# Gate and up by seven block products in tapped PSUM chains, token pairs outermost

## The chip, the cores and the metric

The kernel runs on one core of one Trainium2 chip. The metric is the time of one execution on the device in microseconds (us); three runs of the kernel before gave 2370.25, 2370.45 and 2370.57 us, so the median is 2370.45 us. The core's engines work side by side, each on its own queue of instructions, in order: TensorE (PE, with its weight loads as PEld), VectorE (DVE), ScalarE (ACT), GpSimd (POOL) and SyncE (SP), which here issues the DMAs. They wait for each other through semaphores.

## The reference

A mixture of eight routed experts and one shared expert is added to its input. There are 16 sequences of 256 tokens, so 4096 tokens, of width 256, and each expert is 1024 wide.

```python
E, B, S, D, F = (8, 2, 256, 256, 1024)   # the real B is 16
g = jnp.einsum('bsd,edf->ebsf', h, Wg)
u = jnp.einsum('bsd,edf->ebsf', h, Wu)
expert_outs = jnp.einsum('ebsf,efd->ebsd', jax.nn.silu(g) * u, Wd)
expert_output = jnp.einsum('be,ebsd->bsd', gating_probs, expert_outs)
shared = jnp.einsum('bsf,fd->bsd', jax.nn.silu(h @ Sg) * (h @ Su), Sd)
sg = shared_gate_prob[:, :, None]
x = x + (1.0 - sg) * expert_output + sg * shared
```

All arrays are float32. The gate g and the up projection u use the same input h; silu(g) * u goes through the down projection, and the result is weighted with one number for each sequence and expert.

## The kernel before

**Tiles.** The 4096 tokens are 8 tiles of 512 tokens, held transposed (128 partitions of the width, two halves of it, 512 tokens). Nine experts (eight and the shared one) each have 8 chunks of 128 of their 1024 columns. One tile times one chunk is a unit of the work; there are 9 x 8 x 8 = 576 of them.

**Precision.** Each operand is kept as a high part (`w_hi`, `x_hi`, `h_hi`) and the rest (`w_lo`, `x_lo`, `h_lo`), each in the type fp32r. A `product` (lines 170 to 174) is three matmuls of a 128x128 stationary block with 512 moving columns: hi·hi, hi·lo and lo·hi.

**A unit** has two products for the gate (the two halves of the width), two for up, and two for down (the two halves of the output): 6 products, 18 matmuls. ACT applies silu to the gate in PSUM (`unit`, line 294), DVE multiplies with up in PSUM (line 397), ACT makes `h_hi` (line 300), DVE makes `h_lo` (line 404), and PE uses both in `down`.

**Order.** The loops run over the experts outermost and over the tiles within. PE's queue is written out by hand: `down` of a unit stands ahead of gate and up of the unit two later (`tile`, lines 210 to 219 and after), with two PSUM banks each for gate and up and four for down. The down sums of one tile and one expert stay in PSUM for 8 units; DVE then adds them to `acc` with the coefficient (`add_tile`, line 384). The weights of an expert are loaded once, 72 loads of 384 KB in all; ACT makes their hi (line 284) and DVE their lo (line 368) once each, 8 pairs per expert. POOL works only at the start: it makes hi and lo of the tiles 1 to 7 (lines 161 and 163). SP issues all large DMAs.

Of the kernel before, what the change touches and what calls it, by code (L numbers as in the profile page):

```python
# [5 lines left out]
F32 = mybir.dt.float32  # L25
# [6 lines left out]
S_BUFS = 2  # L32
H_BUFS = 4


def moe_kernel(nc, xT, w, probs, shared_gate, out):
# [4 lines left out]
    D = DC * P  # L41
    HALVES = BATCH // TILES
    SEQ = TOKENS // HALVES
    assert EXPERTS == ROUTED + 1 and W_COLS == 3 * D and TILES % 2 == 0 and HALVES * TILES == BATCH
    UNITS = TILES * CHUNKS
    PAIRS = (TILES - 2) // 2


    FREED = 2


    LEAD = 3
    GATE = slice(0, D)
    REST = slice(D, 3 * D)

    with ExitStack() as ctx:
# [8 lines left out]
        x_hi = sb("x_hi", [P, TILES, DC, TOKENS], F32R)  # L65
        x_lo = sb("x_lo", [P, TILES, DC, TOKENS], F32R)
        w_raw = sb("w_raw", [P, CHUNKS, W_COLS])
        w_hi = sb("w_hi", [P, CHUNKS, W_COLS], F32R)
        w_lo = sb("w_lo", [P, CHUNKS, W_COLS], F32R)
        silu = sb("silu", [P, S_BUFS, TOKENS])  # L70
        h = sb("h", [P, S_BUFS, TOKENS])
        h_hi = sb("h_hi", [P, H_BUFS, TOKENS], F32R)
        h_lo = sb("h_lo", [P, H_BUFS, TOKENS], F32R)
# [6 lines left out]
        gate_ps = ctx.enter_context(nc.psum_tensor("gate_ps", [P, 2, TOKENS], F32))  # L80
        up_ps = ctx.enter_context(nc.psum_tensor("up_ps", [P, 2, TOKENS], F32))
        down_ps = ctx.enter_context(nc.psum_tensor("down_ps", [P, 2, DC, TOKENS], F32))

        w0_gate_loaded = sem("w0_gate_loaded")
        x0_loaded = [sem(f"x0_loaded{c}") for c in range(DC)]
        w_loaded = [sem(f"w_loaded{k}") for k in range(CHUNKS)]
        x_loaded = [sem(f"x_loaded{t}") for t in range(1, TILES)]
        gates_loaded = sem("gates_loaded")
        stored = sem("stored")
        w_hi_done = sem("w_hi_done")  # L90
        w_split = sem("w_split")
        w0_gate_hi_done = sem("w0_gate_hi_done")
        w0_gate_split = sem("w0_gate_split")
        x0_hi_done = [sem(f"x0_hi_done{c}") for c in range(DC)]
        x0_split = sem("x0_split")
        x_hi_done = sem("x_hi_done")
        x_split = sem("x_split")

        gate_done = sem("gate_done")
        up_done = sem("up_done")  # L100
        down_done = sem("down_done")
        silu_done = sem("silu_done")
        prod_done = sem("prod_done")
        h_hi_done = sem("h_hi_done")
        h_split = sem("h_split")
        tile_added = sem("tile_added")
        last_sums = sem("last_sums")
        last_added = sem("last_added")
# [5 lines left out]


        @block.sync
        def _(sp):
            def load_weights(e, k):
                sp.dma_start(w_raw[:, k, :], w[e, k]).then_inc(w_loaded[k], 16)

            def load_tokens(t):
                sp.dma_start(acc[:, t], xT[t]).then_inc(x_loaded[t - 1], 16)


            sp.dma_start(acc[:, 0, 0, :], xT[0, :, 0, :]).then_inc(x0_loaded[0], 16)
            sp.dma_start(w_raw[:, 0, GATE], w[0, 0, :, GATE]).then_inc(w0_gate_loaded, 16)
            for c in range(1, DC):
                sp.dma_start(acc[:, 0, c, :], xT[0, :, c, :]).then_inc(x0_loaded[c], 16)
            sp.dma_start(w_raw[:, 0, REST], w[0, 0, :, REST]).then_inc(w_loaded[0], 16)
            for k in range(1, CHUNKS):  # L130
                load_weights(0, k)
            for t in range(1, TILES):
                load_tokens(t)
            with sp.Fori(1, EXPERTS) as e:
                for k in range(CHUNKS):

                    sp.wait_ge(w_split, (e - 1) * CHUNKS + k + 1)
                    sp.dma_start(
                        w_raw[:, k, :], w[bass.ds(e, 1), k, :, :].rearrange("a p c -> (a p) c")
                    ).then_inc(w_loaded[k], 16)  # L140
            with sp.Fori(0, TILES - 1) as t:

                sp.wait_ge(tile_added, (EXPERTS - 1) * TILES + 1 + t)
                sp.dma_start(
                    out[bass.ds(t, 1)].rearrange("a p c n -> (a p) c n"),
                    acc[:, bass.ds(t, 1)].rearrange("p a c n -> p (a c) n"),
                ).then_inc(stored, 16)
            for c in range(DC):

                sp.wait_ge(last_added, c + 1)  # L150
                sp.dma_start(out[TILES - 1, :, c, :], acc[:, TILES - 1, c, :]).then_inc(stored, 16)
            sp.wait_ge(stored, 16 * (TILES - 1 + DC))


        @block.gpsimd
        def _(pool):
            pool.dma_start(probs_sb[:], probs.partition_broadcast(P)).then_inc(gates_loaded, 16)
            pool.dma_start(shared_sb[:], shared_gate.partition_broadcast(P)).then_inc(gates_loaded, 16)
            for t in range(1, TILES):
                pool.wait_ge(x_loaded[t - 1], 16)  # L160
                nc.gpsimd.tensor_copy(x_hi[:, t], acc[:, t]).then_inc(x_hi_done, 1)
                pool.wait_ge(x_hi_done, t)
                nc.gpsimd.tensor_tensor(
                    x_lo[:, t], acc[:, t], x_hi[:, t].bitcast(F32), ALU.subtract
                ).then_inc(x_split, 1)


        @block.tensor
        def _(pe):
            def product(out_ps, k, cols, moving_hi, moving_lo, start, stop):  # L170

                nc.tensor.matmul(out_ps, w_hi[:, k, cols], moving_hi, start=start, stop=False)  # L172
                nc.tensor.matmul(out_ps, w_hi[:, k, cols], moving_lo, start=False, stop=False)  # L173
                return nc.tensor.matmul(out_ps, w_lo[:, k, cols], moving_hi, start=False, stop=stop)  # L174

            def tile_x(t):

                if isinstance(t, int):
                    return [(x_hi[:, t, c, :], x_lo[:, t, c, :]) for c in range(DC)]
                return [  # L180
                    tuple(x[:, bass.ds(t, 1), c, :].rearrange("p a n -> p (a n)") for x in (x_hi, x_lo))
                    for c in range(DC)
                ]

            def first_gate():

                g = gate_ps[:, 0, :]
                for c in range(DC):
                    cols = slice(c * P, (c + 1) * P)
                    if c == 0:  # L190
                        pe.wait_ge(w0_gate_hi_done, 1)
                    pe.wait_ge(x0_hi_done[c], 1)
                    nc.tensor.matmul(g, w_hi[:, 0, cols], x_hi[:, 0, c, :], start=(c == 0), stop=False)
                    pe.wait_ge(x0_split, c + 1)
                    nc.tensor.matmul(g, w_hi[:, 0, cols], x_lo[:, 0, c, :], start=False, stop=False)
                pe.wait_ge(w0_gate_split, 1)
                for c in range(DC):
                    cols = slice(c * P, (c + 1) * P)
                    last = nc.tensor.matmul(g, w_lo[:, 0, cols], x_hi[:, 0, c, :], start=False, stop=(c == DC - 1))
                last.then_inc(gate_done, 1)  # L200

            def gate_up(e, T, k, x, wait_banks=True, only_up=False):


                pe.wait_ge(w_split, e * CHUNKS + k + 1)
                sides = ((gate_ps, 0, gate_done, silu_done), (up_ps, D, up_done, prod_done))
                for ps, column0, done, used in sides[1:] if only_up else sides:
                    if wait_banks:

                        pe.wait_ge(used, T * CHUNKS + k - 1)  # L210
                    for c in range(DC):
                        cols = slice(column0 + c * P, column0 + (c + 1) * P)
                        last = product(ps[:, k % 2, :], k, cols, *x[c], start=(c == 0), stop=(c == DC - 1))
                    last.then_inc(done, 1)

            def down(T, k, parity, very_last=False):


                pe.wait_ge(h_split, T * CHUNKS + k + 1)
                for c in range(DC):  # L220
                    cols = slice(2 * D + c * P, 2 * D + (c + 1) * P)
                    last = product(
                        down_ps[:, parity, c, :], k, cols, h_hi[:, k % H_BUFS, :], h_lo[:, k % H_BUFS, :],
                        start=(k == 0), stop=(k == CHUNKS - 1),
                    )
                    if very_last and c < DC - 1:
                        last.then_inc(last_sums, 1)
                last.then_inc(down_done, 1)
# [301 lines left out]
```

## Time and profile before

| what | value |
|---|---|
| median of the timed runs | 2370.45 us |
| span of the profiled execution, first to last instruction | 2368.9 us |
| outside that span, by the median | 1.55 us |
| PE busy | 2355.2 us, 99% |
| DVE busy | 973.8 us, 41% |
| ACT busy | 757.2 us, 32% |
| POOL busy | 30.3 us, 1% |
| granted TensorE clock, mean | 1.000 |

The profiled execution has no time of its own beside its span; the runs were timed apart, within 0.32 us of each other. Matmuls overlap, so the row of one shows 0.39 us while they start 0.227 us apart: the distance of the starts is what one costs. A row of a DVE or ACT instruction likewise overlaps the next on its engine by 0.08 to 0.10 us.

### The profile page before, as it was taken

How to read it: one execution, taken by the hardware profiler on the slowest of the kernel's cores; microseconds unless marked ns; L12 is line 12 of the kernel's file. 1: busy time of each engine (PE TensorE's matmuls, PEld its weight loads, DVE VectorE, ACT ScalarE, POOL GpSimd, SP SyncE). 2: the span in 40 equal slices, each digit the busy share in tenths (PEclk: the TensorE clock that was granted, in tenths of full speed). 3: DMA queues.
4: the chain of work that ended last, by engine and by line, in shares of the span. 5: the costliest groups of instructions: out<-in, count | busy, mean ns of one | idle time of the engine just before them, and what ended most of it. 6: DMA issues, size and time to landing. Idle time of an engine off the chain costs nothing.

```text
span 2368.9 us, 29088 instructions
## 1 busy us (share of the span) xinstructions
PE 2355.2 (99%) x10368; PEld 1947.9 (82%) x10368; DVE 973.8 (41%) x1385; ACT 757.2 (32%) x1228; POOL 30.3 (1%) x20
## 2 busy tenths in 40 slices
PE   8999999999999999999999999999999999999999
PEld 6888888888888888888888888888888888888887
DVE  6333533344333533343333433353334433353333
ACT  3222322233222322233233323242223322232222
POOL 5000000000000000000000000000000000000000
PEclk9999999999999999999999999999999999999999
DMA  5000100000000100010000100010000100000000
GB/s 179 1 0 0 54 0 0 0 27 27 0 0 0 53 0 0 0 41 12 0 0 3 51 0 0 0 53 0 0 0 20 33 0 0 0 0 18 18 9 27
DMA packets 13183, 36.98 MB, mean 16 GB/s; under 512 B 1488, under 2 KB 1632, under 8 KB 13168
## 3 DMA queue, kind: packets, MB, share of 16 engines
q1 hardware_dynamic: 13104, 36.71, 4.7%
q0 software_dynamic: 64, 0.07, 0.1%
q8 instruction: 9, 0.15, 0.0%
q14 instruction: 6, 0.05, 0.0%
HBM read 32.58 MB, written 4.19 MB: 16 GB/s over the span
## 4 chain that ended last, share of the span: by engine, by line
PE 98%; DVE 1%; DMA 0%; ACT 0%; issue 0%; SPq 0%; DVEq 0%
PE down_ps L172 11%; PE up_ps L174 11%; PE up_ps L172 11%; PE up_ps L173 11%; PE down_ps L174 11%; PE down_ps L173 11%; PE gate_ps L174 11%; PE gate_ps L172 11%; PE gate_ps L173 11%; DMA acc<-xT 0%; DVE w_lo L368 0%; DVE h_lo L404 0%; DVE h L397 0%; ACT h_hi L300 0%; DVE acc L485 0%
## 5 line engine op out<-in xcount | busy, mean ns | idle before, releaser
L397 DVE TENSOR_TENSOR h<-silu,up_ps 128x512 f32<-128x512 f32 x576 | 396.0, 687 | 1067.0 <-PE up_ps L174 1066.3
L300 ACT CAST h_hi<-h 128x512 fp32r<-128x512 f32 x576 | 357.4, 621 | 872.7 <-DVE h L397 872.7
L294 ACT ACTIVATE silu<-gate_ps 128x512 f32<-128x512 f32 x576 | 344.5, 598 | 724.3 <-PE gate_ps L174 724.1
L404 DVE TENSOR_TENSOR h_lo<-h,h_hi 128x512 fp32r<-128x512 f32 x576 | 407.7, 708 | 311.8 <-ACT h_hi L300 303.2
L172 PE MATMUL down_ps<-h_hi,w_hi 128*128 128x512 f32 x1152 | 448.7, 390 | 1.0 <-DVE h_lo L404 0.8
L172 PE MATMUL up_ps<-x_hi,w_hi 128*128 (+1 forms) x1152 | 448.6, 389 | 0.0
L173 PE MATMUL up_ps<-x_lo,w_hi 128*128 (+1 forms) x1152 | 448.6, 389 | 0.0
L174 PE MATMUL up_ps<-x_hi,w_lo 128*128 (+1 forms) x1152 | 448.6, 389 | 0.0
L173 PE MATMUL down_ps<-h_lo,w_hi 128*128 128x512 f32 x1152 | 448.2, 389 | 0.0
L174 PE MATMUL down_ps<-h_hi,w_lo 128*128 128x512 f32 x1152 | 448.2, 389 | 0.0
L172 PE MATMUL gate_ps<-x_hi,w_hi 128*128 (+1 forms) x1150 | 447.6, 389 | 0.0
L173 PE MATMUL gate_ps<-x_lo,w_hi 128*128 (+1 forms) x1150 | 447.4, 389 | 0.0
L174 PE MATMUL gate_ps<-x_hi,w_lo 128*128 (+1 forms) x1150 | 447.4, 389 | 0.0
L172 PEld LDWEIGHTS down_ps<-h_hi,w_hi 128*128 128x128 f32 x1152 | 216.3, 188 | 47.7 <-DVE h_lo L404 3.1
L173 PEld LDWEIGHTS up_ps<-x_lo,w_hi 128*128 128x128 f32 x1152 | 216.6, 188 | 45.0
L174 PEld LDWEIGHTS up_ps<-x_hi,w_lo 128*128 128x128 f32 x1152 | 216.6, 188 | 45.0
L172 PEld LDWEIGHTS up_ps<-x_hi,w_hi 128*128 128x128 f32 x1152 | 216.6, 188 | 44.9
L174 PEld LDWEIGHTS down_ps<-h_hi,w_lo 128*128 128x128 f32 x1152 | 216.3, 188 | 44.9
L173 PEld LDWEIGHTS down_ps<-h_lo,w_hi 128*128 128x128 f32 x1152 | 216.3, 188 | 44.7
L173 PEld LDWEIGHTS gate_ps<-x_lo,w_hi 128*128 128x128 f32 x1150 | 216.1, 188 | 44.9
L172 PEld LDWEIGHTS gate_ps<-x_hi,w_hi 128*128 128x128 f32 x1150 | 216.1, 188 | 44.8
L174 PEld LDWEIGHTS gate_ps<-x_hi,w_lo 128*128 128x128 f32 x1150 | 215.9, 188 | 44.8
(31 smaller groups left out, 281.9 us busy)
## 6 DMA issues: line engine op xcount, KB each, us to landing
w_raw<-w SPq DMA_DIRECT2D x71, 384.0 KB, 3.0
acc<-xT SPq DMA_DIRECT2D x7, 512.0 KB, 11.7
outT<-acc SPq DMA_DIRECT2D x7, 512.0 KB, 2.6
acc<-xT SPq DMA_DIRECT2D x2, 256.0 KB, 5.5
outT<-acc SPq DMA_DIRECT2D x2, 256.0 KB, 2.0
w_raw<-w SPq DMA_DIRECT2D x1, 256.0 KB, 8.3
w_raw<-w SPq DMA_DIRECT2D x1, 128.0 KB, 2.7
probs_sb<-probs POOLq DMA_DIRECT2D x1, 64.0 KB, 5.7
```

The costliest lines, as they stand in the source:

```text
L172: nc.tensor.matmul(out_ps, w_hi[:, k, cols], moving_hi, start=start, stop=False)
L173: nc.tensor.matmul(out_ps, w_hi[:, k, cols], moving_lo, start=False, stop=False)
L174: return nc.tensor.matmul(out_ps, w_lo[:, k, cols], moving_hi, start=False, stop=stop)
L294: nc.scalar.activation(silu[:, k % S_BUFS, :], gate_ps[:, k % 2, :], ACT.Silu).then_inc(silu_done, 1)
L300: nc.scalar.copy(h_hi[:, k % H_BUFS, :], h[:, k % S_BUFS, :]).then_inc(h_hi_done, 1)
L397: nc.vector.tensor_tensor(h[:, k % S_BUFS, :], silu[:, k % S_BUFS, :], up_ps[:, k % 2, :], ALU.mult).then_inc(prod_done, 1)
L404: nc.vector.tensor_tensor(h_lo[:, k % H_BUFS, :], h[:, k % S_BUFS, :], h_hi[:, k % H_BUFS, :].bitcast(F32), ALU.subtract).then_inc(h_split, 1)
```

## The change

The tokens are now taken in pairs of tiles. With two tiles and two halves of the width, the inputs of a pair are a 2x2 matrix of blocks B, and the four weight blocks of a chunk (gate and up, two halves each) a 2x2 matrix of blocks A. Their product needs eight block products in the plain way; it is now made from seven (a scheme of Strassen's kind) in the form of Winograd, of four sums of weight blocks (S1 to S4) and four of input blocks (T1 to T4).

A unit is now one chunk for a pair of tiles: 7 products for gate and up and 4 for down, 33 matmuls. There are 4 x 9 x 8 = 288 units. The token pairs are the outermost loop, so the weights are loaded, summed and split anew for each of the four pairs: 288 loads and 288 splits. A split has now 9 blocks of 128 columns (1152) and not 6 (768).

Chains of products stay open in PSUM and are read ("tapped") in between: ACT copies P1, P5 and a later state of the first chain to SBUF (`tap_p1`, `tap_p5`, `tap_u2`), PE goes on adding to the same bank, and DVE adds tap and bank to gate of tile 0, gate of tile 1 and up of tile 1; up of tile 0 is the end of the chain. `h` gets its coefficient at once (two instructions of 256 columns for each tile), so the down sums of all experts stay in four PSUM banks for the 72 units of a pair and are added to `acc` once. POOL makes the four weight sums two units ahead, `h_lo` of both tiles, and the input sums and `x_lo` of the next pair; ACT makes all hi parts; DVE makes `w_lo`.

```diff
-            def product(out_ps, k, cols, moving_hi, moving_lo, start, stop):
...
+            def weight_sums(n, s):
+                step(S1, A21, A22, ALU.add)
+                step(S3, A11, A21, ALU.subtract)
+                pool.wait_ge(w_sums, 4 * n + 1)
+                step(S2, S1, A11, ALU.subtract)
+                pool.wait_ge(w_sums, 4 * n + 3)
+                step(S4, A12, S2, ALU.subtract)
...
+                def steady(e, k, new_x=False):
+                        h_lo_of(1, n - 1)
+                        h_lo_of(0, n - 1)
...
+                        weight_sums(n + AHEAD, s)
+                    if new_x:
+                        for form in X_AT.get(k, ()):
+                            x_form(g + 1, form)
+                        for form in X_AT.get(k - 1, ()):
+                            x_form_lo(g + 1, form)
...
+            def unit(g, e, k, first=False):
+                pe.wait_ge(w_lo_done, n + 1)
+                after(pe, h0_done, n - 1)
+                product(chain, s, A11, *x(B11), start=True, stop=True).then_inc(p1_done, 1)
+                after(pe, gate1_done, n)
+                product(p53_ps[:], s, S1, *x(T1), start=True, stop=True).then_inc(p5_done, 1)
+                after(pe, gate0_done, n)
+                product(p2_ps[:], s, A12, *x(B21), start=True, stop=True).then_inc(p2_done, 1)
+                pe.wait_ge(p1_tapped, n + 1)
+                product(chain, s, S2, *x(T2), start=False, stop=True, goes_on=True).then_inc(p6_done, 1)
+                    pe.wait_ge(h_lo_done[1], n)
+                    down(before[0], (k - 1) % CHUNKS, 1, start=opens, stop=closes)
+                pe.wait_ge(p5_tapped, n + 1)
+                product(p53_ps[:], s, S4, *x(B22), start=False, stop=True, goes_on=True).then_inc(p3_done, 1)
+                pe.wait_ge(u2_tapped, n + 1)
+                product(chain, s, S3, *x(T3), start=False, stop=True, goes_on=True).then_inc(p7_done, 1)
+                    pe.wait_ge(h_lo_done[0], n)
+                    down(before[0], (k - 1) % CHUNKS, 0, start=opens, stop=closes)
+                pe.wait_ge(up1_done, n + 1)
+                product(chain, s, A22, *x(T4), start=False, stop=True, goes_on=True).then_inc(p4_done, 1)
...
+            def weight_hi(n, s):
+                act.wait_ge(w_sums, 4 * (n + 1))
+                after(act, down_done[0], n - SLOTS + 1)
+                nc.scalar.copy(w_hi[:, s, :], w_raw[:, s, :]).then_inc(w_hi_done, 1)
...
+            def unit(g, e, k):
+                    h0(*before, n - 1)
+                gate0(n)
+                    weight_lo(n + 1, (k + 1) % SLOTS)
+                gate1(n)
+                up_of_1(n, k)
+                h1(g, e, n)
+                if closes and before[0] >= 0:
+                    for t in (1, 0):
+                        add(before[0], t, n - 1)
```

In ACT's queue two units of the kernel before read as follows, in the middle of an expert (`unit`, lines 294 and 300).

```order
L294 ACTIVATE silu<-gate_ps 128x512 [waits prod_done,gate_done]
L300 CAST h_hi<-h 128x512 [waits down_done,prod_done]
L290 REGISTER_ALU
L294 ACTIVATE silu<-gate_ps 128x512 [waits prod_done,gate_done]
L300 CAST h_hi<-h 128x512 [waits down_done,prod_done]
```

One unit of the changed kernel in the same queue, while no input blocks are made:

```order
L355 COPY tap_p1<-chain_ps 128x512 [waits gate0_done,p1_done]
L358 COPY tap_p5<-p53_ps 128x512 [waits up1_done,p5_done]
L347 CAST h_hi<-h 128x512 [waits down0_done,h0_done]
L363 COPY tap_u2<-chain_ps 128x512 [waits gate1_done,p6_done]
L366 ACTIVATE silu<-gate 128x512 [waits h0_done,gate0_done]
L323 ISA
L325 CAST w_hi<-w_raw 128x1152 [waits down0_done,w_sums]
L374 ACTIVATE silu<-gate 128x512 [waits h1_done,gate1_done]
L347 CAST h_hi<-h 128x512 [waits down1_done,h1_done]
```

The silu of tile 1 (L374) now stands behind `w_hi` of the unit two later, which waits for POOL's sums (`w_sums`), and the first tap of the next unit stands behind the `h_hi` of tile 1.

In POOL's queue, in the loop over the experts, one unit of the changed kernel (before, the queue has 7 pairs of L161 and L163 and nothing after them):

```order
L182 TENSOR_TENSOR h_lo<-h,h_hi 128x512 [waits down1_done,h1_hi_done]
L182 TENSOR_TENSOR h_lo<-h,h_hi 128x512 [waits down0_done,h0_hi_done]
L214 ISA
L168 TENSOR_TENSOR w_raw<-w_raw 128x128 [waits w_loaded0]
L168 TENSOR_TENSOR w_raw<-w_raw 128x128
L174 ISA
L168 TENSOR_TENSOR w_raw<-w_raw 128x128 [waits w_sums]
L176 REGISTER_ALU
L168 TENSOR_TENSOR w_raw<-w_raw 128x128 [waits w_sums]
```

The four sums (L168) stand behind both `h_lo` (L182) of the unit before.

In DVE's queue a unit of the changed kernel, beginning with its first tile-0 product of the unit before (before, a unit there has L397 and L404):

```order
L412 SCALAR_TENSOR_TENSOR h<-silu,coef,chain_ps 128x256 [waits h0_lo_done,silu0_done,p4_done]
L412 SCALAR_TENSOR_TENSOR h<-silu,coef,chain_ps 128x256
L439 TENSOR_TENSOR gate<-tap_p1,p2_ps 128x512 [waits silu0_done,p1_tapped,p2_done]
L430 REGISTER_ALU
L431 TENSOR_TENSOR w_lo<-w_raw,w_hi 128x1152 [waits w_hi_done]
L445 TENSOR_TENSOR gate<-tap_u2,p53_ps 128x512 [waits silu1_done,u2_tapped,p3_done]
L451 TENSOR_TENSOR up1<-tap_p5,chain_ps 128x512 [waits h1_done,p5_tapped,p7_done]
L424 SCALAR_TENSOR_TENSOR h<-silu,coef,up1 128x256 [waits h1_lo_done,up1_done,silu1_done]
L424 SCALAR_TENSOR_TENSOR h<-silu,coef,up1 128x256
```

`w_lo` (L431) moved from once per chunk and expert to once per unit, between the two gates.

## Rows read from the trace of the kernel before

**Rows 1.** The page: span, and busy time of each engine (share, count)
```profile
span 2368.9 us, 29088 instructions
PE 2355.2 (99%) x10368; PEld 1947.9 (82%) x10368; DVE 973.8 (41%) x1385; ACT 757.2 (32%) x1228; POOL 30.3 (1%) x20
```

**Rows 2.** Busy time by stretches: length, engines, then clock, DMA share, GB/s
```profile
1000.00:1500.00 500.00, 500.00 (x2207) 414.15 (x2207) 206.29 (x294) 161.12 (x261) 0.00 (x0) 1.00 0.04 13
```

**Rows 3.** Timeline in mid-run (start, duration, engine, instruction, idle before and releaser)
```profile
1002.54 0.39 PE L172 MATMUL up_ps<-x_hi,w_hi 128*128 x1
...
1002.74 0.60 ACT L294 ACTIVATE silu<-gate_ps 128x512 f32<-128x512 f32 x1 [1.30 <-PE gate_ps L174]
...
1004.10 0.69 DVE L397 TENSOR_TENSOR h<-silu,up_ps 128x512 f32<-128x512 f32 x1 [1.94 <-PE up_ps L174]
...
1004.82 0.62 ACT L300 CAST h_hi<-h 128x512 fp32r<-128x512 f32 x1 [1.49 <-DVE h L397]
```

**Rows 4.** Groups of instructions: busy us, mean ns of one, idle before
```profile
L397 DVE TENSOR_TENSOR h<-silu,up_ps 128x512 f32<-128x512 f32 x576 | 396.0, 687 | 1067.0 <-PE up_ps L174 1066.3 <-DVE coef L442 0.7
L300 ACT CAST h_hi<-h 128x512 fp32r<-128x512 f32 x576 | 357.4, 621 | 872.7 <-DVE h L397 872.7
L485 DVE SCALAR_TENSOR_TENSOR acc<-down_ps,coef,acc 128x256 f32<-128x256 f32 x4 | 1.7, 479 | 1.3 <-PE down_ps L174 1.3
```

**Rows 5.** Timeline of POOL, 19 to 27 us
```profile
19.77 2.40 POOL L163 TENSOR_TENSOR x_lo<-acc,x_hi 128x1024 fp32r<-128x1024 f32 x1
22.11 1.50 POOL L161 CAST x_hi<-acc 128x1024 fp32r<-128x1024 f32 x1
23.70 3.00 POOL L163 TENSOR_TENSOR x_lo<-acc,x_hi 128x1024 fp32r<-128x1024 f32 x1
```

**Rows 6.** Timeline of DVE in the same stretch
```profile
19.81 2.91 DVE L404 TENSOR_TENSOR h_lo<-h,h_hi 128x512 fp32r<-128x512 f32 x1 [0.69 <-ACT h_hi L300]
22.64 1.79 DVE L368 TENSOR_TENSOR w_lo<-w_raw,w_hi 128x768 fp32r<-128x768 f32 x1
24.35 0.68 DVE L397 TENSOR_TENSOR h<-silu,up_ps 128x512 f32<-128x512 f32 x1
25.71 1.53 DVE L404 TENSOR_TENSOR h_lo<-h,h_hi 128x512 fp32r<-128x512 f32 x1 [0.69 <-ACT h_hi L300]
```

**Rows 7.** Instructions that touch w_raw: duration ns min/median/max, first and last start
```profile
L284 ACT CAST w_hi<-w_raw x71: 827/833/838, 11.5 to 2111.1; 128x768 fp32r<-128x768 f32 x71
L368 DVE TENSOR_TENSOR w_lo<-w_raw,w_hi x71: 957/958/1789, 12.3 to 2112.0; 128x768 fp32r<-128x768 f32 x71
...
L344 ACT CAST w_hi<-w_raw x1: 404/404/404, 4.0 to 4.0; 128x256 fp32r<-128x256 f32 x1
...
L457 DVE TENSOR_TENSOR w_lo<-w_raw,w_hi x1: 418/418/418, 11.1 to 11.1; 128x256 fp32r<-128x256 f32 x1
```

**Rows 8.** Timeline at the start, POOL and PE (POOL's first work and PE at the lower clock)
```profile
0.25 0.10 POOL L523 MEMSET const-float32-0.0<- 128x1 f32 x1 [0.25 <-issue]
...
13.08 0.63 PE L173 MATMUL up_ps<-x_lo,w_hi 128*128 128x512 f32 x1
...
13.51 0.63 PE L174 MATMUL up_ps<-x_hi,w_lo 128*128 128x512 f32 x1
```

**Rows 9.** Timeline of PE at a wait for h_lo
```profile
26.76 0.39 PE L174 MATMUL up_ps<-x_hi,w_lo 128*128 128x512 f32 x1
27.30 0.50 PE L172 MATMUL down_ps<-h_hi,w_hi 128*128 128x512 f32 x1 [0.15 <-DVE h_lo L404]
27.64 0.40 PE L173 MATMUL down_ps<-h_lo,w_hi 128*128 128x512 f32 x1
```

**Rows 10.** The chain that ended last, first 30 us: start, us, what
```profile
1.66 8.13 DMA acc<-xT
```

**Rows 11.** DMA issues: KB each, median us from issue to landing
```profile
w_raw<-w SPq DMA_DIRECT2D x71, 384.0 KB, 3.0
...
outT<-acc SPq DMA_DIRECT2D x7, 512.0 KB, 2.6
```

## What I predict, and why
> **What bounds the kernel now.** I read the page's busy times first: PE is busy for 2355 of 2369 us, DVE for 41%, ACT for 32%, POOL for 1% [rows 1]. The windows by stretches say the same of mid-run: in 500 us PE starts 2207 matmuls at a granted clock of 1.00, so one costs 500/2207 = 0.2266 us [rows 2]. The reader is to see that nothing but the number of matmuls sets the time: 10368 x 0.2266 = 2349 us, and 20 us of start and end make the span. Then I read the hand-overs, because the change hangs on them. ACT starts 0.20 us after the next product's first matmul [rows 3], so a product is readable 0.20 us after its last matmul's turn; DVE and ACT follow each other after 0.03 us (4.10 + 0.69 to 4.82) [rows 3]. Last I read the only stretch in which POOL works, 19 to 46 us, beside DVE.
>
> **PE's part.** A pair of tiles and a chunk took 36 matmuls, 8.16 us; it now takes 33, 33 x 0.2266 = 7.48 us. Over 288 units that is 2153 us in place of 2349, a gain of 196 us if nothing else binds. So the question is whether the three other engines close a unit in 7.48 us.
>
> **POOL and DVE exclude each other.** In [rows 5] and [rows 6] POOL's x_lo runs from 19.77 to 22.17. DVE's h_lo, normally 0.69 us, starts at 19.81 and ends at 22.72: 0.55 us after POOL. The next one starts at 25.71 and ends at 27.24, 0.54 us after the x_lo that ended at 26.70. The other way too: that x_lo started at 23.70, DVE's w_lo ended at 24.43, and x_lo ended 2.27 us after that, where alone it takes 2.40. So the one waits for the whole of the other, and only the first part of an instruction, 0.13 to 0.15 us, is hidden by the wait. It holds for a DVE instruction with two SBUF inputs; the product with a PSUM input, at 24.35, took its 0.68 us beside x_lo. In the new kernel w_lo and the tile-1 product (silu and up1, both in SBUF) have two SBUF inputs, and POOL works in every unit.
>
> The Trainium skill speaks of this twice, and not alike. Its "Advanced Engine Details and Errata" (VectorE Performance Modes) lets only 2-port Vector modes block GpSimd, and its table has no such mode for tensor_tensor; by that w_lo would block nothing. Its "GPSIMD Engine Reference" (Key points) adds Vector instructions with two SBUF inputs; by that the trace agrees.
>
> **The loop that sets a unit.** ACT's queue puts silu of tile 1 behind w_hi of the unit two later, which waits for POOL's four sums; POOL makes these behind both h_lo of the unit before; h_lo of tile 1 needs h_hi, that needs the tile-1 product, and that needs silu of tile 1 of its own unit. This is a ring with one turn per unit, and its length is the unit's time if it is over 7.48:
>
> 1. h_lo of tile 1 on POOL, 512 columns: half of 2.27, and 0.13 = 1.27 us [rows 5, 6]. (Half of 2.40 is 1.20.)
> 2. w_lo on DVE. Gate 0 needs the first tap, which stands in ACT's queue right behind h_hi of tile 1: tap 0.60, gate 0 0.69 [rows 3, 4]. So w_lo is queued about 1.15 us after h_hi ends, while h_lo of tile 1 runs to 1.35. The h_lo of tile 0 cannot start before its own h_hi, behind two taps, at 1.6 us. So w_lo has the port next. Its length: (958 - 418)/512 = 1.055 ns a column, so 1152 columns take 0.958 + 0.405 = 1.36, less 0.15 hidden: 1.21 us [rows 7].
> 3. h_lo of tile 0, waiting by then: 1.14 us, the half of 2.27.
> 4. Four sums of 128 columns on POOL. The trace has no such small one. By columns alone it would be 2.40/8 = 0.30 us, the low bound. With the 0.13 that a wait hides it is 0.13 + 0.28 = 0.41; a one-column memset takes 0.10 [rows 8], so a fixed part is there. The high bound is DVE's own: 128 columns there are 0.418 - 0.135 = 0.283, and POOL is slower by 2.40/1.23 at 1024 columns (DVE's 1.23 by the slope of item 2): 0.55. I take 0.43, near the 0.41. Two of them wait for POOL's own sum, which costs 0.09 each (23.61 to 23.70), two starts overlap by 0.06: 1.78, with the register rows between them 1.80 us. Bounds 1.26 and 2.28.
> 5. w_hi on ACT, 1152 columns: 0.833 + 384 x 0.429/512 = 1.155; 0.03 to start, less 0.10 of overlap: 1.08 us [rows 7].
> 6. silu of tile 1: 0.60 + 0.03 = 0.63 us [rows 3].
> 7. The tile-1 product, two instructions of 256 columns: 0.479 + 0.40, and 0.03: 0.90 us [rows 4]. The row has one PSUM input, the new one none; that could halve its rate (below).
> 8. h_hi of tile 1, 0.62, and 0.08 to POOL's start: 0.70 us [rows 4].
>
> The sum is 1.27 + 1.21 + 1.14 + 1.80 + 1.08 + 0.63 + 0.90 + 0.70 = 8.73 us. It is over PE's 7.48, so PE waits 1.25 us per unit, above all for the first tap (P6) and a little for h_lo of tile 1; each restart costs it about 0.1 us more (0.34 where 0.227 is usual) [rows 9]. What PE saves is idle time.
>
> The Trainium skill's "GPSIMD Engine Reference" (Elementwise, side by side) gives 4497 ns for 2048 columns; with the trace's 2.40 at 1024 an estimate is 0.30 fixed and 0.56 for a sum, at which the ring would be 9.2 us.
>
> **Weights and queues.** Each unit loads 384 KB, 288 loads for 72. A load is issued when w_lo of the unit four earlier is done and lands 3.0 us later [rows 11]; POOL needs it more than a unit after that. I cost it at nothing; SP has nothing else queued until a pair ends. DVE has about 4.9 us of its own per unit (three additions at 0.61, four half products in 1.75, w_lo 1.36), so it is late only where it waits.
>
> **The ends and the pair changes.** For three pairs, seven units each make input blocks. Each puts an ACT copy of 0.52 us before silu of tile 1; three of these also wait for POOL's input sum, 0.25, 0.25 and 1.1 us (1.27 per sum against w_hi's 1.05). That is 7 x 0.52 + 1.6 = 5.2 us, 16 us in all; POOL's own extra work fits into the 3.4 us that it idles in a unit (items 5 to 8). Head: the second half of x landed at 9.79 [rows 10]; now four such loads and a whole weight chunk stand ahead, so about 10.5; then DVE has some 9 of its 11 input instructions left at 0.61, held up by POOL's first sums, and w_lo 1.36 behind them: PE starts at about 20 us. Tail: product 0.2 + 0.9, h_hi 0.65, h_lo 1.35, down 1.6, add 1.3, store 2.6 [rows 11]: 9 us. So 45 us in all. A unit's break-even is (2370.45 - 1.55 - 45)/288 = 8.07 us.
>
> **The forecast.** 288 x 8.73 = 2514; with 16, 20 and 9 it is 2559 us of span, and with the 1.55 that the median of the runs lies above the span, 2560 us: 8% slower. With the low bounds (sums 1.26, h_lo 1.20) the ring is 8.12 and the time 2385; with the high bound of the sums it is 9.21 and 2700.
>
> **Rivals.**
>
> *The port does not bind the ring: faster.* If w_lo slipped into POOL's 3.4 us of idle time, or did not block POOL, item 2 falls away: 8.73 - 1.21 = 7.52, and with restarts 7.6. Then 288 x 7.6 + 46.5 = 2235 us, 6% faster. It decides from a unit of 8.07 down. Against it stand the three blocked rows [rows 5, 6] and DVE's order, in which w_lo always follows gate 0. For it: a fixed cost of POOL that I overrate would also help. The first page of the Trainium skill named above would give this time.
>
> *The tile-1 product at half rate: slower still.* The trace has no scalar_tensor_tensor with two SBUF inputs. At half rate 512 columns cost 0.54 us more, the ring is 9.27 and the time 2715. The Trainium skill says so in "Vector Engine (DVE) Microarchitecture Reference" (Points that are easy to get wrong): such an instruction with two non-bf16 SBUF sources "halves throughput". No row here shows it; tensor_tensor with two SBUF inputs runs at the rate of one with a PSUM input [rows 4, 6].
>
> *The clock falls.* PE now idles in each unit. At the lower level a matmul costs 0.43 us [rows 8]: 33 of them 14.1 us, 4100 us in all. Against it: after a short idle time PE went on at full rate [rows 9].
>
> **Chances.** The forecast's ring, between its bounds: 70%. Port not in the ring: 13%. Half rate: 12%. Clock: 2%. Something that I don't see, either way: 3%. From these: faster by over 0.2% (about what a measurement can tell from none) 15%, within it 2%, slower 83%. The range of 8 in 10 takes the forecast's own bounds, 2385 to 2700, and a part of the half-rate case: 2375 to 2720.
>
> **What would show it.** The profile after: PE at about 86% with some 1 us of idle time per unit before P6 (the fourth product, into chain_ps), released by ACT's tap. POOL's h_lo (L182) in two kinds, about 1.27 and 2.1 us, the second overlapping a w_lo (L431); the sums (L168) at 0.41 to 0.45; w_lo itself at 1.36 or a little over; ACT idle before w_hi (L325) for POOL. The chain of waits should run through POOL, ACT and DVE and hardly through PE. Wrong would be: PE at 95% and more, sums at 0.30, a w_lo beside a POOL instruction with both at full speed, or L424 at 0.75 us.

## The result, and the profile after

The changed kernel takes 2595.09 us (2594.38 to 2595.99, four runs) against 2370.35 us before: 1.095 times as long, with a 95% interval of 1.093 to 1.096. The forecast was 2560 us, 35 us less. The profile after has a span of 2592.6 us. Its page shows what became of the 864 matmuls that were saved:

```profile
span 2592.6 us, 33278 instructions
PE 2309.5 (89%) x9504; PEld 1744.1 (67%) x9504; DVE 1472.9 (57%) x2334; ACT 1434.7 (55%) x2334; POOL 1534.5 (59%) x1767
```

PE is no longer always busy, and no other engine is either [rows 1]: the mark of a ring of waits. This is one turn of it in the timelines of the changed kernel (start us, duration us; the bracket is the idle time before and who ended it), first POOL, then DVE, then ACT, then PE where it waits:

```profile
1004.03 1.29 POOL L182 TENSOR_TENSOR h_lo<-h,h_hi 128x512 fp32r<-128x512 f32 x1 [3.36 <-ACT h_hi L347]
1005.53 2.15 POOL L182 TENSOR_TENSOR h_lo<-h,h_hi 128x512 fp32r<-128x512 f32 x1 [0.21 <-ACT h_hi L347]
1007.64 1.83 POOL L168 TENSOR_TENSOR w_raw<-w_raw 128x128 f32<-128x128 f32 x4
1012.85 1.28 POOL L182 TENSOR_TENSOR h_lo<-h,h_hi 128x512 fp32r<-128x512 f32 x1 [3.37 <-ACT h_hi L347]
```

```profile
1004.53 0.69 DVE L439 TENSOR_TENSOR gate<-tap_p,p_ps 128x512 f32<-128x512 f32 x1 [0.45 <-issue]
1005.13 1.40 DVE L431 TENSOR_TENSOR w_lo<-w_raw,w_hi 128x1152 fp32r<-128x1152 f32 x1
...
1011.24 0.88 DVE L424 SCALAR_TENSOR_TENSOR h<-silu,coef,up 128x256 f32<-128x256 f32 x2 [2.12 <-ACT silu L374]
```

```profile
1009.51 1.16 ACT L325 CAST w_hi<-w_raw 128x1152 fp32r<-128x1152 f32 x1 [2.90 <-POOL w_raw L168]
1010.57 0.63 ACT L374 ACTIVATE silu<-gate 128x512 f32<-128x512 f32 x1
1012.15 0.62 ACT L347 CAST h_hi<-h 128x512 fp32r<-128x512 f32 x1 [0.95 <-DVE h L424]
```

```profile
1003.27 0.39 PE L260 MATMUL p_ps<-x_hi,w_lo 128*128 128x512 f32 x1
1004.49 0.50 PE L258 MATMUL chain_ps<-x_hi,w_hi 128*128 128x512 f32 x1 [0.84 <-ACT tap_p L355]
...
1005.07 0.39 PE L260 MATMUL chain_ps<-x_hi,w_lo 128*128 128x512 f32 x1
1005.37 0.50 PE L258 MATMUL down_ps<-h_hi,w_hi 128*128 128x512 f32 x1
```

Follow it: h_lo of tile 1 runs from 1004.03 to 1005.32. w_lo was issued at 1005.13 and ends at 1006.53. The h_lo of tile 0 was issued at 1005.53 but ends at 1007.68, 1.15 us after w_lo. The four sums end at 1009.47, w_hi starts at 1009.51, silu at 1010.57, the product at 1011.24, h_hi at 1012.15, and the next h_lo at 1012.85: 8.82 us. PE's fourth product starts 1.22 us after the matmul ahead of it, where 0.227 is usual, released by ACT's first tap.

The waits of the changed kernel (engine and line, who ended them: us in total, times, longest) put numbers to it:

```profile
POOL h_lo L182 <- ACT h_hi L347: 1015.3, 544, 9.6
ACT w_hi L325 <- POOL w_raw L168: 832.3, 286, 3.2
DVE h L424 <- ACT silu L374: 621.7, 286, 4.2
...
PE chain_ps L258 <- ACT tap_p L355: 254.1, 282, 2.8
```

### The profile page after: what moved, and what is told of

The parts are those of the page before. It is cut to its first block and busy times, and to the rows that moved or that the text cites. A ratio compares the mean times of both kernels' runs of the same rounds, so it can differ in the third digit from the quotient of the medians.

```text
span 2592.6 us, 33278 instructions
## 1 busy us (share of the span) xinstructions
PE 2309.5 (89%) x9504; PEld 1744.1 (67%) x9504; DVE 1472.9 (57%) x2334; ACT 1434.7 (55%) x2334; POOL 1534.5 (59%) x1767
## 5 line engine op out<-in xcount | busy, mean ns | idle before, releaser
L182 POOL TENSOR_TENSOR h_lo<-h,h_hi 128x512 fp32r<-128x512 f32 x576 | 993.2, 1724 | 1019.3 <-ACT h_hi L347 1015.3
L325 ACT CAST w_hi<-w_raw 128x1152 fp32r<-128x1152 f32 x288 | 333.5, 1158 | 832.3 <-POOL w_raw L168 832.3
L258 PE MATMUL chain_ps<-x_hi,w_hi 128*128 128x512 f32 x1152 | 481.4, 418 | 273.0 <-ACT tap_p L355 254.1
L424 DVE SCALAR_TENSOR_TENSOR h<-silu,coef,up 128x256 f32<-128x256 f32 x576 | 255.3, 484 | 621.8 <-ACT silu L374 621.7
L168 POOL TENSOR_TENSOR w_raw<-w_raw 128x128 f32<-128x128 f32 x1152 | 509.4, 462 | 30.2 <-DMA w_raw<-w 6.4
L259 PE MATMUL chain_ps<-x_lo,w_hi 128*128 128x512 f32 x1152 | 450.8, 391 | 0.0
L260 PE MATMUL chain_ps<-x_hi,w_lo 128*128 128x512 f32 x1152 | 450.6, 391 | 0.0
L431 DVE TENSOR_TENSOR w_lo<-w_raw,w_hi 128x1152 fp32r<-128x1152 f32 x288 | 404.9, 1406 | 0.0
L258 PE MATMUL p_ps<-x_hi,w_hi 128*128 128x512 f32 x864 | 338.0, 391 | 0.0
L259 PE MATMUL p_ps<-x_lo,w_hi 128*128 128x512 f32 x864 | 337.0, 390 | 0.0
L260 PE MATMUL p_ps<-x_hi,w_lo 128*128 128x512 f32 x864 | 336.7, 390 | 0.0
L412 DVE SCALAR_TENSOR_TENSOR h<-silu,coef,chain_ps 128x256 f32<-128x256 f32 x576 | 249.4, 474 | 0.8 <-PE chain_ps L260 0.8
```

Source lines behind the costliest of these rows:

```text
L168: nc.gpsimd.tensor_tensor(raw[:, cols(dst, dst)], raw[:, cols(a, a)], raw[:, cols(b, b)], op).then_inc(w_sums, 1)
L182: nc.gpsimd.tensor_tensor(h_lo[:, t], h[:, t], h_hi[:, t].bitcast(F32), ALU.subtract).then_inc(h_lo_done[t], 1)
L258: nc.tensor.matmul(bank, w_hi[:, s, c], hi, start=start, stop=False, **on)
L259: nc.tensor.matmul(bank, w_hi[:, s, c], lo, start=False, stop=False, **on)
L260: return nc.tensor.matmul(bank, w_lo[:, s, c], hi, start=False, stop=stop, **on)
L325: nc.scalar.copy(w_hi[:, s, :], w_raw[:, s, :]).then_inc(w_hi_done, 1)
```

## The experiments

The **ring theory** is that of the prediction. Two rivals stood against it. **Port load**: POOL and DVE are simply too busy on what they share, in whatever order. **Chain**: PE loses its time in the tapped chains, since each tap goes through ACT before PE may go on. Each of the first three runs moves one thing in one queue and leaves all work in.

### w_lo out of the ring (e1_wlo_late)

```diff
                 gate0(n)
-                if not isinstance(n, int) or n + 1 <= LAST:
-                    weight_lo(n + 1, (k + 1) % SLOTS)
                 gate1(n)
                 up_of_1(n, k)
+                if not isinstance(n, int) or n + 1 <= LAST:
+                    weight_lo(n + 1, (k + 1) % SLOTS)
                 h1(g, e, n)
```

> The changed kernel with one move in DVE's queue: w_lo of the next unit stands behind the addition of up of tile 1, where DVE idled for silu, and not between the two gates. All work is kept. Ring theory (one turn per unit: h_lo of tile 1, w_lo, h_lo of tile 0, sums, w_hi, silu, product, h_hi; 8.82 us in the trace after): w_lo leaves the ring, 7.6 us are left; but its end now comes close to the next unit's first product on PE, which needs it, so a unit of 7.6 to 8.0 and 2240 to 2370 us. Port-load rival (the port of POOL and DVE is simply busy too long, in whatever order): no change, 2595 within 1%. Chain rival (PE loses its time in the tapped chains themselves, by ACT's tap latency): no change either.

Measured: 2364.03 us (seven runs), 0.997 of the kernel before (0.996 to 0.998), 231 us below the change. In the groups of its profile (busy us, mean ns of one | idle before) POOL's h_lo is no longer blocked:

```profile
L182 POOL TENSOR_TENSOR h_lo<-h,h_hi 128x512 fp32r<-128x512 f32 x576 | 747.1, 1297 | 1022.4 <-ACT h_hi L347 1018.5
L431 DVE TENSOR_TENSOR w_lo<-w_raw,w_hi 128x1152 fp32r<-128x1152 f32 x288 | 400.0, 1389 | 0.0
```

With w_lo between them the mean of an h_lo was 1724 ns, half of them near 1290 and half at 2150. But 231/288 = 0.80 us per unit came back, not the whole 1.21 of item 2. w_lo has left one ring and stands in another. DVE, then PE's first product (P1) and, in the last line, what its weight loads waited for in all:

```profile
1004.27 0.69 DVE L445 TENSOR_TENSOR gate<-tap_u,p_ps 128x512 f32<-128x512 f32 x1 [2.20 <-PE p_ps L260]
1005.56 1.35 DVE L431 TENSOR_TENSOR w_lo<-w_raw,w_hi 128x1152 fp32r<-128x1152 f32 x1
1006.93 0.88 DVE L424 SCALAR_TENSOR_TENSOR h<-silu,coef,up 128x256 f32<-128x256 f32 x2
...
1012.28 0.69 DVE L445 TENSOR_TENSOR gate<-tap_u,p_ps 128x512 f32<-128x512 f32 x1 [2.26 <-PE p_ps L260]
```

```profile
1006.96 0.50 PE L258 MATMUL chain_ps<-x_hi,w_hi 128*128 128x512 f32 x1
```

```profile
PEld chain_ps L258 <- DVE w_lo L431: 138.8, 256, 18.8
```

P1 starts 0.05 us after w_lo ends (1006.91). It and the next 20 matmuls, to the end of P3, release gate 1 at 1012.28. Gate 1 and the addition for up of tile 1 stand ahead of the next w_lo, which starts at 1013.56, 8.00 us after this one; the median from one w_lo to the next is 7.97 us. The tile-1 product (L424) waits behind w_lo too: its silu had ended at 1006.77. That this second ring sets the time is read from the rows; no run takes w_lo out of it.

Both rivals foresaw no change and fall as sole causes.

### The ring cut at silu (e2_silu_first)

```diff
+                act.wait_ge(gate1_done, n + 1)
+                after(act, h1_done, n)
+                nc.scalar.activation(silu[:, 1], gate[:, 1], ACT.Silu).then_inc(silu_done[1], 1)
                 if not isinstance(n, int) or n + AHEAD <= LAST:
                     weight_hi(n + AHEAD, (k + AHEAD) % SLOTS)
...
-                act.wait_ge(gate1_done, n + 1)
-                after(act, h1_done, n)
-                nc.scalar.activation(silu[:, 1], gate[:, 1], ACT.Silu).then_inc(silu_done[1], 1)
                 h_hi_of(1, n, h1_done)
```

> The changed kernel with one move in ACT's queue: silu of tile 1 stands ahead of w_hi of the unit two later (and of the x_hi copies), so it no longer waits for POOL's sums. All work is kept, and DVE's w_lo stays where it was and is still blocked by POOL. Ring theory: the ring is cut at silu; what is left is h_lo, w_lo, h_lo, sums, w_hi, h_hi = 1.29 + 1.21 + 1.15 + 1.79 + 1.10 + 0.70 = 7.24 us, below PE's 7.48, so a unit of 7.5 to 7.8 and 2210 to 2300 us. Port-load rival and chain rival: no change, 2595 within 1%.

Measured: 2215.01 us (four runs), 0.935 of the kernel before (0.933 to 0.936). One instruction moved ahead of another on an engine that is busy 55% of the time is worth 380 us. Both fell again: the taps and the load of the port were as before.

### The sums in POOL's idle time (e3_sums_first)

```diff
+                    if not isinstance(n, int) or n + AHEAD <= LAST:
+                        w_arrived(s, ...)
+                        weight_sums(n + AHEAD, s)
                     if not isinstance(n, int) or n > 0:
                         h_lo_of(1, n - 1)
                         h_lo_of(0, n - 1)
-                    if not isinstance(n, int) or n + AHEAD <= LAST:
-                        w_arrived(s, ...)
-                        weight_sums(n + AHEAD, s)
```

> The changed kernel with one move in POOL's queue: the four weight sums of a unit stand ahead of both h_lo. All work is kept. Ring theory: POOL makes the sums in the 3.4 us in which it idled, w_hi finds them ready, and nothing but PE's 33 matmuls (7.48 us) is left as the longest: 288 x 7.48 + 50 = 2205, at most 2260 us. Port-load rival and chain rival: no change, 2595 within 1%.

Measured: 2205.78 us (four runs), 0.930 of the kernel before (0.929 to 0.932); the expectation was 2205. Its page shows the opposite of a port that is too full:

```profile
span 2204.3 us, 33272 instructions
PE 2167.1 (98%) x9504; PEld 1785.5 (81%) x9504; DVE 1777.1 (81%) x2334; ACT 1486.9 (67%) x2334; POOL 1608.6 (73%) x1767
```

and its groups say that POOL and DVE now block each other more than ever, outside any ring:

```profile
L168 POOL TENSOR_TENSOR w_raw<-w_raw 128x128 f32<-128x128 f32 x1152 | 814.8, 728 | 30.4 <-DMA w_raw<-w 6.6 <-DMA acc<-xT 1.3
L431 DVE TENSOR_TENSOR w_lo<-w_raw,w_hi 128x1152 fp32r<-128x1152 f32 x288 | 677.8, 2354 | 0.0
```

A w_lo takes 2354 ns here, 948 more than in the changed kernel, and a sum 728 for 462. One unit in the timelines, POOL and then DVE, says how:

```profile
1014.03 1.30 POOL L182 TENSOR_TENSOR h_lo<-h,h_hi 128x512 fp32r<-128x512 f32 x1 [0.57 <-ACT h_hi L347]
1015.28 2.96 POOL L168 TENSOR_TENSOR w_raw<-w_raw 128x128 f32<-128x128 f32 x4
```

```profile
1014.13 2.40 DVE L431 TENSOR_TENSOR w_lo<-w_raw,w_hi 128x1152 fp32r<-128x1152 f32 x1
```

w_lo is held until h_lo ends at 1015.33 and ends 1.20 us after it, at 1016.53; the first sum is held by it in turn. The kernel is 389 us faster all the same. That settles the port-load rival. It settles the chain rival too, since all taps are in place and PE is busy for 98%.

### Prices: two sums out, a copy off the ring, a copy on it

The first leaves out S2 and S4 in all but the first four units:

```diff
                 step(S3, A11, A21, ALU.subtract)
+                if not (isinstance(n, int) and n < SLOTS):
+                    return
                 pool.wait_ge(w_sums, 4 * n + 1)
```

> The changed kernel in which all units but the first four leave out two of the four weight sums (S2 and S4; those blocks keep what the first use of the slot left). All orders are kept. It prices item 4 of the ring. Ring theory: two small instructions and two waits on POOL's own semaphore go; the four take 1.79 us in the trace after, the two that are left 0.88, so a unit is 8.82 - 0.91 = 7.9 us and the time 2595 - 262 = 2333 us (2310 to 2360). Port-load rival: the time is not the order's but the port's busy share, 0.9 us of 5.9: 2450 to 2550.

Measured: 2333.06 us (four runs): 262 us less, 0.91 us per unit, to the microsecond what the ring theory gave. That price was read from the trace after; from rounder numbers (1.0 us a unit) I had first written down 2310 us (2280 to 2350) for a form that leaves the two sums out of every unit, and that form has no time.

The other two add the same ACT instruction at two places, with its own tiles:

```diff
                 nc.scalar.activation(silu[:, 0], gate[:, 0], ACT.Silu).then_inc(silu_done[0], 1)
+                nc.scalar.copy(extra_out[:], extra_in[:])        # e5_copy_off
...
                         x_form_hi(g + 1, form)
+                nc.scalar.copy(extra_out[:], extra_in[:])        # e6_copy_on
                 act.wait_ge(gate1_done, n + 1)
```

> The changed kernel with one more ACT instruction in each unit, a copy of 512 columns between two SBUF tiles of its own, right behind silu of tile 0, where ACT then waits 2.9 us for POOL's sums. Ring theory: it lies off the ring, no change, 2595 within 0.5%. Load rival (ACT, at 55%, is simply too slow for the unit): up to 0.52 us a unit, 2745 us. It is one half of a pair with the next run.

Measured: 2593.94 us (four runs), the time of the changed kernel.

> The changed kernel with the same additional copy in each unit, but between w_hi and silu of tile 1, on the ring. Ring theory: its whole pitch comes through, 0.62 - 0.10 = 0.52 us x 288 = 150, so 2745 us (2730 to 2760). Load rival: the same as in the run before. Chain rival (PE's taps): no change in either.

Measured: 2739.35 us (four runs), 145 us more than the run before on the same chip, 0.505 us per unit. ACT's own timeline in e5_copy_off shows why the other copy is free: it ends at 1006.99, and w_hi waits until 1009.38 in any case.

```profile
1005.84 0.63 ACT L368 ACTIVATE silu<-gate 128x512 f32<-128x512 f32 x1
1006.38 0.61 ACT L369 COPY extra_out<-extra_in 128x512 f32<-128x512 f32 x1
1009.38 1.16 ACT L327 CAST w_hi<-w_raw 128x1152 fp32r<-128x1152 f32 x1 [2.40 <-POOL w_raw L170]
```

### An earlier start (e7_head)

On top of e3_sums_first:

```diff
                 lo(B11, x[0][0])
+                weight_lo(0, 0)
                 dve.wait_ge(x_loaded[0][1], 16)
...
             first_x()
-            weight_lo(0, 0)
```

> The changed kernel with POOL's sums ahead of both h_lo (as in e3_sums_first) and, in DVE's queue at the start, w_lo of the first unit right behind x_lo of the first block and not behind all seven. All work is kept. In the trace of e3_sums_first PE's first matmul waits until 18.3 us for that w_lo. It can now start at about 9.9 us, but its next products wait for their x_lo, the last at about 17.5, so not 8 but about 6 us are won: 2200 us against 2206. If the later products wait as long as before, nothing changes.

Measured: 2203.92 us (five runs), 0.930 of the kernel before (0.928 to 0.931). It is the fastest median here, but it ran in another session than e3_sums_first, and 1.9 us between them is at the edge of what can be told. Expected were about 6 us, so most of that did not come. PE starts at 10.02 and not at 18.29 us, and its last product of the first unit starts 3.3 us earlier (22.27 for 25.60): its longest waits are now for ACT's first tap (1.40 us) and for up of tile 1 (2.33 us), which DVE makes only behind the input blocks, the coefficients and the next w_lo. Of the 3.3 us, part is given back, as PE's timeline in e7_head shows:

```profile
22.27 0.50 PE L258 MATMUL chain_ps<-x_hi,w_hi 128*128 128x512 f32 x1 [2.33 <-DVE up L451]
22.61 0.39 PE L259 MATMUL chain_ps<-x_lo,w_hi 128*128 128x512 f32 x1
...
24.07 0.63 PE L260 MATMUL chain_ps<-x_hi,w_lo 128*128 128x512 f32 x1
24.50 0.63 PE L258 MATMUL p_ps<-x_hi,w_hi 128*128 128x512 f32 x1
```

```profile
11.00:13.00 2.00, 1.99 (x6) 0.94 (x4) 2.00 (x4) 1.37 (x3) 2.00 (x3) 1.00 1.03 420
23.00:26.00 3.00, 3.00 (x9) 2.33 (x8) 1.15 (x3) 1.21 (x2) 1.27 (x1) 0.50 0.19 75
```

From 23.2 to 26.2 us the matmuls start 0.43 us apart, the lower of the two levels (1.2 GHz), and the granted clock of that stretch is 0.50. (At the start of this kernel, as of the kernel before [rows 8], they also start 0.43 us apart, but there the profile gives a granted clock of 1.00.) Just ahead of the stretch PE had waited 2.33 us. Some eight matmuls at 0.2 us too much are 1.6 us. That the wait is the cause is argued from the order in time, not tested.

## Why the prediction was right, point by point

**What bounds.** The step from "PE alone" to "a ring of POOL, DVE and ACT" held. The eight items, forecast and read from the turn at 1004 to 1013 us:

| item | forecast | measured |
|---|---|---|
| h_lo of tile 1 | 1.27 | 1.29 |
| w_lo in between | 1.21 | 1.21 |
| rest of h_lo of tile 0 | 1.14 | 1.15 |
| four sums | 1.80 | 1.79 |
| w_hi | 1.08 | 1.10 |
| silu | 0.63 | 0.67 |
| product of tile 1 | 0.90 | 0.91 |
| h_hi, and to POOL | 0.70 | 0.70 |
| unit | 8.73 | 8.82 |

The four sums, the item without a row before, came out at 1.79, near the value taken and not near either bound (1.26 and 2.28): a fixed part is there. That it fits so well is partly luck: one of them has a mean of 462 ns, not 430 (and above the 0.41 to 0.45 named as a sign), and the gaps between them were smaller than I had set them.

**Where 35 us were missed.** 288 x 0.09 = 26 us are in the ring, in steps of 0.01 to 0.04: silu from SBUF takes 0.63 and not the 0.60 of silu from PSUM, POOL's half has a larger fixed part, the product two small hand-overs. The other 9 us are in the 45 for the ends and pair changes, and the distances from one w_lo to the next (median 8.82 us) say where. The forecast had nothing for the end of a pair, where DVE adds its down sums to `acc` ahead of the next product of tile 0:

```profile
668.80 0.88 DVE L424 SCALAR_TENSOR_TENSOR h<-silu,coef,up 128x256 f32<-128x256 f32 x2 [2.64 <-ACT silu L374]
669.60 2.35 DVE L457 TENSOR_TENSOR acc<-down_ps,acc 128x1024 f32<-128x1024 f32 x2
671.86 0.86 DVE L412 SCALAR_TENSOR_TENSOR h<-silu,coef,chain_ps 128x256 f32<-128x256 f32 x2
```

At the last pair change, where no input blocks are made, this unit takes 10.54 us, 1.7 more than the median: 5 us for the three. Nor had it anything for the loop over the experts: one unit in each of its turns takes 9.02 us, which is 32 x 0.20 = 6 us; what these 0.20 are is open. The input blocks cost about 5.5 us per pair, against 5.2 forecast (ACT makes the seven in six units and not in seven; the one with two takes 10.78 us). The start gave 2 us back (PE starts at 18.07 us, 20 forecast).

**POOL and DVE exclude each other.** Right, and in the ring: [rows 5, 6] repeat in every unit (2.15 for 1.29), and e1_wlo_late takes the block away. So the rival in which the port is not in the ring did not happen. The 2235 us that I put on it were too low besides: it let all of item 2 fall away and left item 3 at 1.14. Without w_lo the h_lo of tile 0 has its whole 1.29 us and still waits 0.20 for its own h_hi (e1_wlo_late). Then 1.29 + 1.21 + 1.15 = 3.65 us become 2.78, the unit 7.95 and the time about 2345 us. This is an estimate from those rows; no run has a w_lo in its place that does not block.

**Half rate of the tile-1 product.** It did not happen. 256 columns from two SBUF inputs take 484 ns (L424), with one PSUM input 474 (L412) and 479 before [rows 4]. The sentence of the Trainium skill, "Vector Engine (DVE) Microarchitecture Reference" (Points that are easy to get wrong), does not hold for this form: the measurement decides. Its "GPSIMD Engine Reference" (Key points) on two SBUF inputs is borne out in each unit.

**The clock.** The rival, a clock that stays low because PE idles in each unit, did not happen: from 90 to 650 us it is 1.00, with PE waiting 0.84 us in each unit. But the clock did fall for moments. In the units that make the next pair's input blocks PE waits longer for the first tap, and three times, at 78, 682 and 1365 us, the granted clock was 0.50 for about 3.4 us, beginning less than 1 us after PE had waited 2.80, 1.89 and 2.81 us. Another wait of 2.80 us, at 721 us, was not followed by a fall.

```profile
77.48 0.50 PE L258 MATMUL chain_ps<-x_hi,w_hi 128*128 128x512 f32 x1 [2.80 <-ACT tap_p L355]
721.06 0.50 PE L258 MATMUL chain_ps<-x_hi,w_hi 128*128 128x512 f32 x1 [2.80 <-ACT tap_p L355]
```

```profile
79.00:81.00 2.00, 2.00 (x6) 1.61 (x5) 0.53 (x1) 0.61 (x2) 2.00 (x2) 0.50 0.21 35
90.00:650.00 560.00, 506.60 (x2094) 382.94 (x2093) 319.29 (x506) 310.92 (x506) 327.74 (x383) 1.00 0.15 45
```

PE has time to spare there: the unit with the first fall took 9.56 us, the same unit of the next pair, without one, 9.36.

**PE's share.** 86% forecast, 89% by the page; matmul rows overlap the idle time behind them, so PE's idle time is better read from the unit: 8.82 against 7.48.

## What to carry to other kernels

When work is taken off the bounding engine, write down one turn of every ring through the in-order queues of the others, with the hand-overs and with what a shared port makes one engine wait, and compare its length with the new work of the bounding engine: three engines at 55 to 59% made this kernel 9.5% slower. An instruction that is needed two units later must not stand ahead of one that is needed at once; moving it is free, and here turned 9.5% slower into 6.5% faster (7% with the sums moved instead). To see whether something is on a ring, add the same small instruction once on it and once beside it.

## What the runs showed of the hardware that I had not expected

- DVE at 81% and POOL at 73% with a w_lo held for 1.2 us in every unit cost PE next to nothing (e3_sums_first, 98%): each blocked instruction waited for one instruction of the other engine and no more, and here that cost time only where it lay on the ring.
- PE's granted clock fell to 0.50 for about 3.4 us after single waits of 2.33 us (e7_head) and of 1.89 to 2.81 us (changed kernel, three times), not after every one of them, and it stayed at 1.00 over 560 us with 0.84 us of waiting in every 8.82 us.
- A POOL instruction of 128 columns costs 462 ns and one of 512 columns 1290: 2.16 ns a column and about 0.19 us fixed, which at 1024 columns gives the 2.40 us of [rows 5].
